# Attention's prologue: one normalisation, second batch and values inside the first maxima, PSUM banks handed over singly

## The reference, cut to what matters

```python
# x: (2, 1024, 128), 16 heads of 8, 16 gaussian kernels
k_, v_, q_ = split(layernorm(x) @ w_in.T)
scores = jnp.sum(amplitudes[:, :, None] * jnp.exp(-jnp.abs(sharpness)[:, :, None] * diff * diff), axis=1)
logits = jnp.einsum('bhld,bhmd->bhlm', q, k) * scale + bias[None]   # bias[h, i, j] = scores[h, i - j + L - 1]
attn = jax.nn.softmax(logits, axis=-1)
x = x + jnp.einsum('bhlm,bhmd->bhld', attn, v)
```

## Time and profile before

| | us |
|---|---|
| three runs | 1184.16, 1184.66, 1185.03 (median 1184.66) |
| the profiled execution, its own time | 1184.06 |
| its span | 1182.1 |
| PE, DVE, ACT, Pool busy in the span | 1020.0, 983.5, 719.0, 447.7 |
| first reduction of the maxima (DVE) begins | 46.99 |
| first scores of step 0 (PE) begin | 80.92 |
| exponentials at L1203: busy, idle ahead of them | 248.1, 198.4 |
| Pool's low part of a piece, mean | 1.154 |

### The profile page before, as it was taken

One profiled execution on the slowest core, in us unless ns is written; L12 is line 12 of the kernel. 1 busy time (PEld: TensorE's weight loads), 2 busy tenths in 40 slices (PEclk: granted clock), 3 DMA queues, 4 the chain that ended last, 5 costly groups with the idle time before them and its releaser, 6 DMA issues. The chain is left out here.

```text
span 1182.1 us, 19693 instructions
## 1 busy us (share of the span) xinstructions
PE 1020.0 (86%) x5756; PEld 540.9 (46%) x5756; DVE 983.5 (83%) x2432; ACT 719.0 (61%) x1175; POOL 447.7 (38%) x404
## 2 busy tenths in 40 slices
PE   3559999999999999785999999782877769999998
PEld 1212222222222222264766676541656537666775
DVE  6589999889999986168999999787876689999997
ACT  5116665666666656564777777586333537777775
POOL 4600000000000000013777778515663127777776
PEclk9659999999999999967999999986889879999999
DMA  3740122032012200000000000000000000000001
GB/s 100 255 95 8 61 76 49 16 106 66 15 55 75 57 1 2 1 21 12 20 21 18 22 18 23 3 19 0 1 0 0 21 9 21 22 18 21 19 23 38
DMA packets 56704, 41.66 MB, mean 35 GB/s; under 512 B 23334, under 2 KB 51004, under 8 KB 56636
## 3 DMA queue, kind: packets, MB, share of 16 engines
q1 hardware_dynamic: 54268, 38.18, 12.0%
q10 hardware_dynamic: 2368, 2.63, 0.8%
HBM read 33.12 MB, written 7.47 MB: 34 GB/s over the span
## 5 line engine op out<-in xcount | busy, mean ns | idle before, releaser
L514 POOL TENSOR_TENSOR f_act_low<-f_act,f_act_high 128x512 fp32r<-128x512 f32 x256 | 331.2, 1294 | 151.3 <-ACT f_act_high L471 146.3
L1203 ACT ACTIVATE at_prob<-at_cols 128x1024 f32<-128x1024 f32 x256 | 248.1, 1021 | 198.4 <-PE at_cols L1092 198.4
L1255 DVE CUSTOM_DVE_ANT_0 at_rows<-at_rows,at_table_max 128x512 f32<-128x512 f32 x512 | 340.3, 719 | 33.5 <-PE at_rows L1057 32.3
L471 ACT CAST f_act_high<-f_act 128x512 fp32r<-128x512 f32 x256 | 159.1, 621 | 68.1 <-DVE f_act L591 65.7
L585 DVE TENSOR_TENSOR f_gated<-f_relu,f_work 128x512 f32<-128x512 f32 x256 | 174.3, 681 | 21.3 <-PE f_work L417 15.1
L591 DVE TENSOR_TENSOR f_act<-f_gated,f_work 128x512 f32<-128x512 f32 x256 | 175.8, 687 | 10.2
L478 ACT ACTIVATE f_relu<-f_work 128x512 f32<-128x512 f32 x256 | 152.9, 597 | 32.1 <-PE f_work L362 30.7
L360 PE MATMUL f_work<-f_x_high,f_wu_high 128*128 128x512 f32 x256 | 148.4, 580 | 2.7 <-DVE f_wu_low L573 2.1
L1057 PE MATMUL at_rows<-at_k_stack,at_q_stack 48*128 48x512 bf16 x512 | 104.7, 405 | 39.9 <-DVE at_maxima L1255 38.4
L1104 PE MATMUL at_pv<-at_prob,at_v_stack 128*32 128x512 f32 x1024 | 136.4, 605 | 0.6 <-ACT at_prob L1203 0.6
L1092 PE MATMUL at_cols<-at_table_cols,flip_sum 128*64 128x512 f16 x1024 | 136.4, 387 | 0.0
(11 more groups left out here) (274 smaller groups left out, 1393.8 us busy)
## 6 DMA issues: line engine op xcount, KB each, us to landing
at_table_cols<-bias_rows SPq DMA_DIRECT2D x32, 248.0 KB, 5.1
at_table_max<-bias_rows SPq DMA_DIRECT2D x12, 480.0 KB, 4.3
f_wu<-in_L_ffn_up_w_dram SPq DMA_DIRECT2D x64, 64.0 KB, 2.0
f_wd<-in_L_ffn_down_w_dram SPq DMA_DIRECT2D x64, 64.0 KB, 1.8
at_q_stack<-q_parts SPq DMA_DIRECT2D x28, 96.0 KB, 2.4
at_k_stack<-k_parts SPq DMA_DIRECT2D x24, 96.0 KB, 3.9
at_table_max<-bias_rows ACTq DMA_DIRECT2D x4, 480.0 KB, 5.8
k_parts<-at_parts SPq DMA_DIRECT2D x2, 768.0 KB, 5.4
```

The lines of the kernel that those rows point to most:

```text
L471: nc.scalar.copy(act_h[:, j % 4, :], act[:, j % 4, :]).then_inc(act_high, 1)
L514: nc.gpsimd.tensor_tensor(act_l[:, k, :], act[:, k, :], act_h[:, k, :].bitcast(F32), ALU.subtract).then_inc(act_low, 1)
L1203: act(prob[:, S % 2, 2 * hp:2 * hp + 2, :], s2[:, hp, :, :], ACT.Exp).then_inc(exp_done, 1)
L1255: nc.vector.tensor_tensor_reduce(out=slot, in0=slot, in1=t_max[:, 2 * p.hp + j, c:c + BANK][:, ::-1], scale=1.0, scalar=-3.0e38, op0=ALU.a ...
```

## The change

- **Statistics and norm.** The statistics of the first quarter are taken ahead of the sign changes of the bias parameters. All 16 tiles share one variance and one square root, which stands on ACT behind both squares and the weight copies. DVE normalises batch 0, makes `amp_of`, copies the first two turned quarters, then normalises batch 1. Pool's memset of `at_k_stack` waits for all 16 tiles, as it did.
- **First batch.** ACT takes `high_part(0)` between the two gaussians. The bias matmul uses bank 2 of `at_rows`, and the turned quarters use banks 0 and 1.
- **Second batch and values.** PE's projections 4 to 7 and the value matmuls leave the place ahead of the maxima. They are handed out one item behind each pair (four projections, then eight half quarters of values) through `second_batch()`. ACT's copies of the values, which stood ahead of the loads of the q stack and `at_table_max`, now follow them. Of pieces 4 to 7, ACT makes a float32 copy (`whole`) and the high part; Pool does both subtractions and the middle part's rounding, which DVE did. `whole` and `rest` share memory with `prob`, so ACT's first exponential waits for `low_ready`.
- **Single banks.** `fills` counts banks and no longer pairs; each of a pair's two matmuls waits for its own bank and reports it, and so does each reduction.
- **Numbers.** `AHEAD` goes from 22 to 20, and the first `turn_maxima` comes after 17 pairs (18 before). So the last pair of a phase falls in the step S % 8 = 5 (4 before), while `turn_maxima` stays at S % 8 = 6.

```diff
-AHEAD = 22
-TURN_FIRST_AFTER = PHASE_PAIRS + 2
+AHEAD = 20
+TURN_FIRST_AFTER = PHASE_PAIRS + 1
...
         self.start[key] = self.n
         self.n += slots
-        self.fills += 1
-        self.filled[key], self.freed[key] = self.fills, self.n
+        self.end[key] = self.n
...
                 for n in range(KINDS // 2, KINDS):
-                    low_part(n)
+                    pool.wait_ge(high_ready, n + 1)
+                    tt(whole[:, n % 4, :], whole[:, n % 4, :], part(n, 0), ALU.subtract).then_inc(rest_ready, 1)
+                    pool.wait_ge(rest_ready, n - 3)
+                    nc.gpsimd.tensor_copy(part(n, 1), whole[:, n % 4, :]).then_inc(mid_ready, 1)
+                    pool.wait_ge(mid_ready, n + 1)
+                    tt(part(n, 2), whole[:, n % 4, :], part(n, 1), ALU.subtract).then_inc(low_ready, 1)
...
-                pe.wait_ge(xnT_ready, NQ)
-                for g in range(NQ):
-                    values(g)
-                project(2)
-                project(3)
+                def second_batch():
+                    for n in range(KINDS // 2, KINDS):
+                        pe.wait_ge(proj_read, n - 3)
+                        project(n)
+                        yield
+                    for g in range(NQ):
+                        if g:
+                            pe.wait_ge(high_ready, KINDS // 2 + g)
+                        for k in range(QT):
...
                 def rows_pair(n):
-                    if at + 2 > SLOTS:
-                        pe.wait_ge(slots_free, at + 2 - SLOTS)
                     for j in range(2):
...
-                    last.then_inc(fills, 1)
+                        if at + j >= SLOTS:
+                            pe.wait_ge(slots_free, at + j + 1 - SLOTS)
+                        mm(s1[:, (at + j) % SLOTS, :], q_st[r, p.b, p.lh, p.hp, p.lbq * P:(p.lbq + 1) * P],
+                           k_st[r, p.b, p.hp, p.mh * BANK:(p.mh + 1) * BANK], start=True, stop=True).then_inc(fills, 1)
...
+                more = second_batch()
                 for n in range(AHEAD):
                     rows_pair(n)
+                    if n:
+                        next(more, None)
                     if n + 1 == TURN_FIRST_AFTER:
                         pe.wait_ge(m.turn_made, TURN_MADE)
                         turn_maxima(0)
-                pe.wait_ge(proj_read, KINDS)
+                for _ in more:
+                    pass
+                pe.wait_ge(v_copied, NQ)
+                pe.wait_ge(high_ready, KINDS)
...
-                norms[0].scalar_root(a)
+                square(1)
...
-                square(1)
-                norms[1].scalar_root(a)
-                for g in range(HG):
-                    gaussian(g)
-                for n in range(KINDS // 2):
+                norm.scalar_root(a)
+                gaussian(0)
+                high_part(0)
+                gaussian(1)
+                for n in range(1, KINDS // 2):
                     high_part(n)
...
                 for n in range(KINDS // 2, KINDS):
-                    high_part(n)
+                    a.wait_ge(proj_done, n + 1)
+                    nc.scalar.copy(whole[:, n % 4, :], proj_bank(n)).then_inc(whole_ready, 1)
+                    nc.scalar.copy(part(n, 0), proj_bank(n)).then_inc(high_ready, 1)
```

More of the change, by code:

```diff
@@ L676, in __init__ @@
     def __init__(self):
-        self.start, self.filled, self.freed = {}, {}, {}
-        self.n = self.fills = 0
+        self.start, self.end, self.n = {}, {}, 0
         for n in range(AHEAD):
@@ L712, in __init__, with vector_stats @@
         self.norm = m.sem(f"{tag}_xn_ready")
-    def vector_stats(self, v, loaded):
-        for t in self.tiles:
-            if t % QT == 0:
-                v.wait_ge(loaded[t // QT], 16)
+    def vector_stats(self, v, loaded, q):
+        v.wait_ge(loaded[q], 16)
+        for t in range(QT * q, QT * (q + 1)):
             self.m.row_stats(t).then_inc(self.stat, 1)
@@ L799, in attention @@
         onorm = sb("onorm", [P, QT, G4, HD])
-        norms = [RowNorm(m, f"at{b}", xn, b * LT, LT) for b in range(BATCH)]
+        norm = RowNorm(m, "at", xn, 0, NT)
         w_loaded, small_loaded = sem("w_loaded"), sem("small_loaded")
@@ L909, in send_maxima @@
                 def send_maxima(phase):
-                    sp.wait_ge(slots_free, slots.freed["maxima", phase])
+                    sp.wait_ge(slots_free, slots.end["maxima", phase])
                     b, lh = phase // 2 % 2, phase % 2
@@ L927, in _ @@
                             if p.b == 1 and p.lh == 1 and p.lbq == LT // 2 - 1 and p.mh == 1:
-                                sp.wait_ge(slots_free, slots.freed["pair", p.n])
+                                sp.wait_ge(slots_free, slots.end["pair", p.n])
                                 load_max_tables(sp, g + 1, p.hp)
@@ L1029, in _ @@
                 pe.wait_ge(w_ready, 2)
-                project(0)
-                project(1)
+                for n in range(KINDS // 2):
+                    project(n)
                 pe.wait_ge(amp_ready, 1)
@@ L1143, in _ @@
                 act = nc.scalar.activation
[L1144 removed]
+                for t, src in ((off, offsets), (shp, sharpness), (amp, amplitudes)):
                     a.dma_start(t[:], src.rearrange("(g h) k -> (h k) g", g=HG),
@@ L1177, in _ @@
                     a.dma_start(bias_hi[:, c * BANK:(c + 1) * BANK], b_hi[32 * c:32 * c + HEADS, :]).then_inc(b_hi_out, 16)
-                for g in range(NQ):
-                    a.wait_ge(v_done, g + 1)
-                    bank = (s1[:, 1, :], s1[:, 2, :], pv[:], s1[:, 0, :])[g]
-                    nc.scalar.copy(v_nat[:, g * QT:(g + 1) * QT, :].rearrange("p t d -> p (t d)"), bank).then_inc(v_copied, 1)
                 a.wait_ge(stored[0], 16 * STORES)
@@ L1188, in _ @@
                 for n in range(KINDS // 2, KINDS):
-                    high_part(n)
+                    a.wait_ge(proj_done, n + 1)
+                    nc.scalar.copy(whole[:, n % 4, :], proj_bank(n)).then_inc(whole_ready, 1)
+                    nc.scalar.copy(part(n, 0), proj_bank(n)).then_inc(high_ready, 1)
+                for g in range(NQ):
+                    a.wait_ge(v_done, g + 1)
+                    nc.scalar.copy(v_nat[:, g * QT:(g + 1) * QT, :].rearrange("p t d -> p (t d)"), v_bank(g)).then_inc(v_copied, 1)
+                a.wait_ge(low_ready, KINDS)
                 def take_outputs(phase):
@@ L1193, in take_outputs @@
                     if phase:
-                        a.wait_ge(fills, slots.filled["out", phase - 1])
+                        a.wait_ge(fills, slots.end["out", phase - 1])
                     nc.scalar.copy(oT[:], pv[:]).then_inc(oT_ready, 1)
@@ L1250, in pair_maxima @@
                         v.wait_ge(max_tab_in[p.hp], 32 * (p.g + 1))
-                    v.wait_ge(fills, slots.filled["pair", n])
                     c = p.lb * P - p.mh * BANK + L - BANK
@@ L1259, in pair_maxima @@
                     if p.last:
-                        negate_maxima(p.phase, slots.freed["pair", n])
+                        negate_maxima(p.phase, slots.end["pair", n])
                 def negate_maxima(phase, freed):
@@ L1277, in copy_maxima @@
                 def copy_maxima(phase):
-                    v.wait_ge(fills, slots.filled["maxima", phase])
+                    v.wait_ge(fills, slots.end["maxima", phase])
                     if phase:
@@ L1287, in add_outputs @@
                     t4 = s1[:, slots.start["out", phase] % SLOTS, :].rearrange("p (t h e) -> p t h e", t=QT, h=G4)
-                    v.wait_ge(fills, slots.filled["out", phase])
+                    v.wait_ge(fills, slots.end["out", phase])
                     if phase:
@@ L1294, in add_outputs @@
                        ALU.mult).then_inc(slots_free, 1)
-                    v.wait_ge(slots_free, slots.freed["out", phase])
+                    v.wait_ge(slots_free, slots.end["out", phase])
                     rows = m.x[:, t0:t0 + QT, c0:c0 + G4 * HD]
```

95 lines of the change are left out of this document (42 added, 53 removed).

## The result

The changed kernel takes 1191.8 us (median of five runs, 1191.5 to 1192.9), the kernel before 1184.7 beside it (1184.2 to 1187.4). The ratio is 1.0058, with a 95% interval of 1.0046 to 1.0071: slower by 7 us. The profiled execution took 1191.47 us, its span is 1189.7 (before: 1182.1). Forecast were 1194.3 and a range of 1185 to 1200. Direction, range and the larger term are right; the smaller term, step 0, has the wrong sign.

The account below looks back on a forecast made before the run. PE was taken to bound the steps and DVE the prologue, with SP's queue setting step 0 after the change. 1184.06 + 2.5 (step 0) + 7.1 (phases) = 1193.7, given as 1194.3; range 1185 to 1200.

Parts of the forecast that it names:

- the larger term: Ends of phases in the attention steps: fourteen turns and a fifteenth cost +7.1 us together, between +4 and +10.
- the smaller term, step 0: Prologue: step 0's scores wait for maxima queued on SP and begin at 83.4, 2.5 us later; -1 to +7.5.
- First reduction: Prologue, start of the maxima on DVE: begins at 40.9, 6.1 us earlier; between 40.0 and 42.
- the second table load landed some 5 us after its issue: Loads before the first reduction: this landing time put the second table load at about 40.8, 44.4 before.
- Pool's chain: Second batch on Pool: four pieces at 3.5 us each, 14.2 us, last low part ending at 59.3.
- The end of a phase: Turn in the attention steps: PE waits for the negation, a step takes 4.45 us, each phase end costs 0.45 more.
- The last turn: Fifteenth turn, in steps without pairs left: waits 1.1 us, less the slack of an ACT-bound step, taken as 0.8.
- DVE's gain of 10 us: Prologue pairs: DVE done at about 70.5, a gain of 10 us not cashed because step 0 waits for SP's queue.
- The first: Rival: SP's queue isn't step 0's bound and phases cost nothing; 1174, or 1181.0 with the phases' 7.1; chance 0.09.
- the second: Rival: the turn costs nothing (1186.6), or step 0 comes at 78 (1188.3); chance 0.17.
- The third: Rival: waits between a pair's two matmuls cost PE 0.1 to 0.2 us a pair; 1218 to 1241; chance 0.12.
- The estimate worked out from the figure of the Trainium skill: Attention steps: reports of packed matmuls follow one another, 236 x 0.026 = 6 us more, 1200; left out of the sum.

Follow-up runs that it names:

- a_max_first: The changed kernel with SP sending the first maxima ahead of the second batch's k and q stacks; 1190.6 us.
- c_selects: The changed kernel with Pool's two long selects moved into its idle time, ahead of its second-batch work; 1193.0 us.
- a_ahead22: The changed kernel with the lead put back to 22 pairs and the first turn after 18; 1186.1 us.
- c_lead21: The changed kernel with a lead of 21 pairs and the first turn after 18; 1185.8 us.
- b_banks: The kernel before with only the single banks, each bank waited for and reported by itself, lead 22; 1181.1 us.
- d_best: The changed kernel with lead 21, selects in Pool's idle time, and SP's `b_lo` stores and column tables behind the first batch's stores; 1177.7 us.
- b_ahead20: The kernel before with only the lead set to 20 and the first turn after 17 pairs; 1189.0 us.
- d_warm: b_banks plus two throw-away matmuls behind each of the last 14 pairs before step 0; 1181.3 us.

## Why the prediction was right or wrong

- **First reduction: 40.9 forecast, 42.02 measured.** The parts were stored as early as said (k load at 32.92 for 33.4), and ACT issued the q loads with it. But the step "the second table load landed some 5 us after its issue" took the landing of before for granted. In a window that holds all four table loads, they now landed after 7.0 us (median) where they took 5.8, and the q loads after 4.4 for 2.4: ACT's q loads now leave at 32.93, in the same moment as SP's k loads. No experiment separated them again, so that cause is argued, not shown.
- **Pool's chain: 3.5 us a piece forecast, 3.02 measured.** The rounding, for which I had no row, took 0.61 us, below my floor of 0.8; the two subtractions took the 1.15 of the earlier trace rows; and Pool's two waits for itself took 0.06 and 0.08 us where I had 0.17 each. That price was misread too: its row counts 14 instructions and not 16, which would make it 0.19. It began at 46.64, 1.5 later than forecast, since projection 4 came at 43.37 at half clock and ACT's first of two copies at 45.48. It was luck that both errors nearly cancel: the last low part ended at 58.76 for 59.3.
- **SP and step 0: +2.5 us forecast, -0.3 measured.** This is the term that failed; the sum is 2.2 too high (1193.7 for 1191.47), 2.8 from here and -0.6 from the rest. The mechanism is the one named: ready maxima stood behind tables and stacks and PE was idle (a_max_first and c_selects show it from both sides). The size was wrong. From the last low part to the first table load it took 5.3 us, not 7.3 (8.9 in the earlier trace rows). Before, the DMA was full there (share 1.05 to 1.06 from 48 to 54, with the stores of all three parts in it) and the two stores of the low parts landed 5.9 and 6.6 us after their issue; now its share had fallen to 0.28 at 56 to 58, ahead of them, and they landed after 3.6 and 3.7. That the emptier DMA is the reason is argued from these numbers and wasn't tested apart. From there to the maxima 8.9 us were forecast and 8.89 measured. And from the issue of the maxima to the scores I had 7.9 us (75.5 to 83.4); it was 7.6 (72.97 to 80.61). Within it, 1.5 us between the end of the large loads and the maxima's landing had no row; from the end of the DMA's work to the scores it was about 0.9. So the error of 2.8 is 2.0 in front of the tables, 0.5 in the chain and 0.3 behind the issue. The time that the DMA needed after the tables' issue was right: its share was still 1.09 at 76 to 78 us and 0.83 at 78 to 80.

```profile
76.00:78.00 2.00, 0.00 (x0) 0.00 (x0) 0.90 (x4) 0.00 (x0) 0.00 (x0) 0.50 1.09 206
78.00:80.00 2.00, 0.00 (x0) 0.00 (x0) 0.00 (x0) 0.00 (x0) 0.00 (x0) 0.50 0.83 161
80.00:82.00 2.00, 1.39 (x7) 0.32 (x9) 0.00 (x0) 0.00 (x0) 0.00 (x0) 0.50 0.00 0
```

  The maxima landed when the last of the large loads had. That fits the rule cited from the Trainium skill (DMA: Bandwidth & Descriptors, "Queues, rings and completion order"), that a queue's descriptors are consumed in ring order. The distances from the issue of the maxima to scores that waited for them agree with it: 7.64, 7.21 (a_ahead22), 7.16 (c_selects) and 7.07 (c_lead21) behind tables and stacks, 5.16 behind the tables alone (a_max_first). In b_banks (4.67) and d_best (3.36) PE had no wait for the maxima, so these two are only upper bounds of their way.
- **The end of a phase: +0.45 us forecast, +0.45 measured** (26.45 for 26.00, fourteen times), with the turn's wait at 1.01 for 1.09 and a step of 4.46 for 4.45. The count from the rows of the last pair to the end of the negation was exact because every piece of it stood in the earlier trace rows. The last turn cost 1.24 (26.50 for 25.26 in the last eight steps) where I took 0.8. I gave it the slack of a step bound by ACT, and there was none: it now stands in the first step without pairs (471.29 to 475.14), in which PE has no wait for ACT. Before, that first step took 2.65 us (462.24 to 464.89), and the wait of 0.29 for ACT came in the one behind it, with the turn. So the whole 1.09 of the turn's wait counts. The remaining 0.15 is in part the one step more with pairs, priced at 0.03: it takes 3.06 us, late steps without pairs 2.98, and the 3.03 that I read as an ordinary one was the step that holds the last turn. Together +7.5 for +7.1.
- **DVE's gain of 10 us, "not cashed".** It shrank first, since the pairs began 1.1 us late and the negation lost 3.8 us to Pool's selects: DVE's first turned maxima were there at 71.62, only 3.0 us earlier than before (74.60), and its last reduction ahead of step 0 ended at 76.8 where I had 70.5. Nothing of that showed, as forecast, because the queue was later still. Single banks do cost nothing in the steps, and in the prologue of the kernel before, where DVE did set step 0, they are most of its 5.7 us (b_banks).
- **Rivals.** The first asked for SP not to be the bound: refuted by a_max_first and c_selects. Of the second, the half on the turn is refuted by a_ahead22 and b_ahead20. Its other half comes nearest in step 0's time, but not by its mechanism, and 80.61 lies between its 78 and the forecast's 83.4. The third, waits between a pair's matmuls: b_banks has the 3.06 us step. The estimate worked out from the figure of the Trainium skill (TensorE: Matmul & The Clock Gate, "The cost: per-tile semaphore tail"), 6 us in 236 pairs, doesn't show in the steps, whose 3.06 us are the same with one and with two reports a pair.

The upper end of the range was added up with 8.4 us for the phases, a number that no line of the prediction gives; its own late end was +10, which would make it 1202.

The sum of the trace: 1184.06 - 0.25 (first products) + 7.48 (from them to the last) + 0.18 (the remainder) = 1191.47.

## What to carry over

A lead between two hand-written streams isn't a smooth dial: count in which place of the consumer's step the producer's last piece falls, and move it by one pair rather than by two. When work is moved from one engine to another, follow it to the queue that waits for it: here a queue in a fixed order held everything behind the slowest piece. A lead of 21 took back the loss of 7 us (1185.8 for 1185.9 beside it); reordering the issues (tables early, nothing behind the late piece but what needs it), together with moving the selects, then gained 8. A gain in front of the first dense stretch is only worth what the granted clock leaves of it.

## What the runs showed that was not expected

- A VectorE rounding of 128x16 elements took 3.99 us beside a Pool select of 128x4096 (4.1 us each), and 0.17 without it; the instructions of the same kind just ahead of the select's start took 0.17 to 0.33. The reductions with their operand in PSUM that ran beside the second select took 0.69 to 0.73, as everywhere else. The same instruction took 3.99 in a_ahead22, a_max_first and c_lead21 too, and 0.17 where the selects ran elsewhere (c_selects, d_best). The Trainium skill (SBUF — State Buffer, "SBUF: two separate sides") says that the port pair shared by the two engines is an exclusive lock: of a GpSimd instruction and a VectorE instruction that uses the pair (one in a two-port mode, or one with two SBUF inputs beside a GpSimd instruction that reads SBUF), the one that starts first has it for the whole instruction, and the other fully blocks. The trace agrees in time: the select began at 66.16, the rounding at 66.26, and the rounding ended at 70.25, when the first select's 4.1 us were about over. Here the loser was an instruction of 0.17 us. In which mode the rounding ran, no trace shows.
- A small transfer of maxima took 7.6 us from its issue to the matmul that waited for it behind the tables and the stacks, and at most 3.4 with the DMA nearly idle (d_best), where no matmul waited for it.
- Pool rounds 128x512 from float32 to bf16 in 0.61 us and subtracts the same size in 1.15.
- The granted clock rose at about 84 us in the kernel before, with step 0 at 80.9, and at about 84.5 in b_banks, with step 0 at 75.2; with added matmuls ahead of step 0 it rose at about 79 (d_warm), and at about 76.4 in d_best, which has none, with step 0 at 73.2. And in a_ahead22, where PE was busier from 74 to 78 us than in the changed kernel (3.7 us against 1.5), it rose only at about 88.4, later than there (84.4). What decides the moment stays open.
